# Key and query projections change places between slots, and value evacuations go ahead of a copy, in a decoder layer's cross-attention

## The reference

```
x = layernorm(x + self_attention(x))            # 16 heads of 64, no mask
x = layernorm(x + cross_attention(x, ctx))      # 16 heads of 16, ctx is 8 x 375 x 256, one mask 112 x 375
x = layernorm(x + ffn(x))                       # 8 experts of hidden 512, top-1 by argmax, plus one shared expert

# cross_attention
q = heads(x @ Wq.T + bq); k = heads(ctx @ Wk.T + bk); v = heads(ctx @ Wv.T + bv)
scores = where(mask == 0, -1e10, q k^T / 4); out = softmax(scores) v
return out @ Wo.T + bo
```

## Time and profile before

| | |
|---|---|
| median of 3 runs | 441.21 us (440.41 to 441.44) |
| profiled execution, its own time | 441.44 us |
| span of its trace | 439.7 us |
| TensorE busy (matmuls) | 415.9 us, 95% of the span |
| TensorE busy (weight loads) | 296.5 us, 67% |
| VectorE busy | 245.2 us, 56% |
| ScalarE busy | 194.1 us, 44% |
| GpSimd busy | 50.5 us, 11% |
| TensorE's granted clock, mean | 0.996 |

### The profile page before, as it was taken

How to read it: one execution, slowest core, us unless ns; L and a number is a source line. 1 busy time by engine, 2 the same in 40 slices (tenths; PEclk the granted TensorE clock), 3 DMA queues, 4 the chain that set the end, 5 groups by cost and what they waited for, 6 DMA issues and landing times.

```text
span 439.7 us, 8960 instructions
## 1 busy us (share of the span) xinstructions
PE 415.9 (95%) x3125; PEld 296.5 (67%) x3126; DVE 245.2 (56%) x724; ACT 194.1 (44%) x580; POOL 50.5 (11%) x77
## 2 busy tenths in 40 slices
PE   8999999999999978999999999999989998999992
PEld 7766868788686755777776677667665474666661
DVE  1275756756566565667575666667763452234442
ACT  1163352434426445677567666667673101011110
POOL 3010010101101001000010101010100045212222
PEclk9999999999999999999999999999999999999998
DMA  8998000000000013040404040920000013122210
GB/s 255 363 388 241 1 1 1 0 1 2 1 1 0 1 37 144 1 180 1 180 2 180 12 170 13 364 92 1 1 2 1 1 49 108 46 63 68 58 44 33
DMA packets 15241, 34.22 MB, mean 78 GB/s; under 512 B 2381, under 2 KB 9150, under 8 KB 13920
## 3 DMA queue, kind: packets, MB, share of 16 engines
q1 hardware_dynamic: 13952, 30.70, 20.0%
q0 software_dynamic: 1104, 2.76, 1.8%
q10 hardware_dynamic: 144, 0.23, 0.2%
HBM read 27.24 MB, written 6.70 MB: 77 GB/s over the span
## 4 chain that ended last, share of the span: by engine, by line
PE 66%; issue 23%; DVE 6%; ACT 2%; SPq 1%; DMA 0%; POOLq 0%; POOL 0%; DVEq 0%; ACTq 0%
PE bank L434 9%; PE bank L635 7%; PE bank L504 6%; PE bank L448 6%; PE bank L617 4%; PE bank L880 4%; PE bank L856 4%; PE bank L532 3%; PE bank L491 3%; PE bank L862 3%; PE bank L465 3%; PE bank L526 3%; PE bank L477 3%; PE bank L651 3%; PE bank L518 1%
## 5 line engine op out<-in xcount | busy, mean ns | idle before, releaser
L1232 DVE CUSTOM_DVE_ANT_0 p<-bank,mask 112x375 f32<-112x375 f32 x128 | 62.7, 545 | 38.6 <-PE bank L617 38.6
L996 ACT ACTIVATE p<-p,nm 112x375 f32<-112x375 f32 x128 | 74.8, 609 | 6.0 <-DVE nm L1232 6.0
L635 PEld LDWEIGHTS bank<-ident,p 112*125 112x125 f32 x384 | 48.9, 187 | 22.8 <-issue 13.7
L1003 ACT ACTIVATE pT<-bank 125x336 f32<-125x336 f32 x96 | 42.8, 447 | 46.1 <-PE bank L635 46.1
L635 PE MATMUL bank<-ident,p 112*125 112x112 f32 x384 | 58.8, 286 | 0.9
L434 PE MATMUL bank<-x2T,arena 128*128 128x224 f32 x256 | 53.9, 359 | 0.0
L939 ACT ACTIVATE p<-bank,nm 112x112 f32<-112x112 f32 x128 | 43.6, 366 | 18.6 <-DVE nm L1106 18.6
L434 PEld LDWEIGHTS bank<-x2T,arena 128*128 128x128 f32 x256 | 47.4, 194 | 0.6 <-DMA x2T<-in_xT 0.4
L349 POOL TENSOR_TENSOR rstd<-veps,minus_half 128x1 f32<-128x1 f32 x14 | 7.7, 549 | 297.2 <-DVE veps L1132 297.2
L1099 DVE TENSOR_SCALAR arena<-bank 128x448 f32<-128x448 f32 x32 | 20.0, 624 | 26.5 <-PE bank L434 26.5
L617 PE MATMUL bank<-kT,qz 32*112 32x375 f32 x256 | 28.8, 517 | 3.5 <-ACT x2T L965 2.1
(11 more groups left out here) (140 smaller groups left out, 598.0 us busy)
## 6 DMA issues: line engine op xcount, KB each, us to landing
arena<-in_ug SPq DMA_DIRECT2D x8, 1024.0 KB, 5.8
arena<-in_dn SPq DMA_DIRECT2D x8, 512.0 KB, 7.7
mid<-in_ctxT SPq DMA_DIRECT2D x8, 375.0 KB, 3.1
slots_s<-blank SPq DMA_DIRECT2D x14, 128.5 KB, 3.4
arena<-in_wqk SPq DMA_DIRECT2D x7, 256.0 KB, 4.9
slots_x<-blank SPq DMA_DIRECT2D x14, 128.0 KB, 6.9
p<-slots_s SPq DMA_DIRECT2D x9, 128.5 KB, 2.1
kT<-slots_x SPq DMA_DIRECT2D x9, 128.0 KB
```

The costliest lines, as they stand in the source:

```text
L635: mm = pe.transpose(PE_T2[r][0:SK, t * S:(t + 1) * S], p2[i % RING][:, t * SK:(t + 1) * SK], ident[0:S, 0:S])
L996: act.activation(p2[i % RING], p2[i % RING], ACT.Exp, bias=nm2[:, i % H:i % H + 1], scale=-1.0).then_inc(exp2, 1)
L1003: act.activation(pT2[0:SK, i % RING], PE_T2[r][0:SK, 0:KT * S].rearrange("p (k n) -> p k n", k=KT), ACT.Copy).then_inc(pt2_act, 1)
L1232: v.tensor_tensor_reduce(p2[i % RING], PE_S2[r][0:S, 0:S2], bias[:], 1.0, 3e38, ALU.add, ALU.min, accum_out=nm2[:, i % H:i % H + 1]).then_ ...
```

## The change

Four edits, all in the cross-attention, and all of order. In batches 2 and 4 TensorE's query projection moves from place 2 of (b,1) to place 0, and VectorE's evacuation of it goes ahead of the maximum of strip 3. The second key half moves from place 0 of (b,1) to place 2, in batches 2 and 4 behind a wait for the query's evacuation. On ScalarE the evacuation of the second key half moves from the middle of (b,1) to the front of (b,2). On VectorE what `between(n, 3)` holds, which is the value evacuations (and in slot (0,0) the first part of a layernorm), goes ahead of `evac_pt2`.

```diff
--- before.py
+++ after.py
@@ -713,18 +713,19 @@
                     else:
                         pe.wait_ge(y2, b - 2)
                     project_k(0, b + 1)
-                if (g, place) == (1, 0) and 1 <= b < B - 1:
+                if (g, place) == (1, 0) and b in (2, 4):
                     pe.wait_ge(k_sb, (b + 1) * KC + 1)
-                    project_k(1, b + 1)
+                    project_q(b // 2 + 1)
                 if (g, place) == (1, 1) and b >= 3:
                     turn_x2(b - 3)
-                if (g, place) == (1, 2) and b in (2, 4):
-                    pe.wait_ge(k_sb, (b + 2) * KC)
-                    project_q(b // 2 + 1)
-                if (g, place) == (2, 0) and b >= 1:
+                if (g, place) == (1, 2) and 1 <= b < B - 1:
                     if b in (2, 4):
                         pe.wait_ge(q_sb, b // 2 + 2)
-                    elif b + 1 < B:
+                    else:
+                        pe.wait_ge(k_sb, (b + 1) * KC + 1)
+                    project_k(1, b + 1)
+                if (g, place) == (2, 0) and b >= 1:
+                    if b + 1 < B:
                         pe.wait_ge(k_sb, (b + 2) * KC)
                     else:
                         pe.wait_ge(y2, B - 3)
@@ -1008,8 +1009,8 @@
                 b, g = n // GROUPS, n % GROUPS
                 if b == 0 and g >= 2:
                     evac_x1(g + 2)
-                if g == 1 and 1 <= b < B - 1:
-                    evac_k(0, b + 1)
+                if g in (1, 2) and 1 <= b < B - 1:
+                    evac_k(g - 1, b + 1)
 
             def between(n, place):
 
@@ -1018,8 +1019,6 @@
                     evac_k(1, 1)
                 if (g, place) == (1, 0) and b == 0:
                     evac_x1(3)
-                if (g, place) == (1, 0) and 1 <= b < B - 1:
-                    evac_k(1, b + 1)
                 if (g, place) == (3, 0) and b == 0:
                     evac_x1(6)
                 if (g, place) == (1, 1) and b >= 3:
@@ -1274,7 +1273,7 @@
                     evac_v(2, b, PE_L2)
                 if (g, place) == (1, 0) and b >= 3:
                     ln2_b(b - 3)
-                if (g, place) == (1, 4) and b in (2, 4):
+                if (g, place) == (1, 2) and b in (2, 4):
                     evac_q(b // 2 + 1)
                 if (g, place) == (2, 2) and b == 0:
                     evac_q(1)
@@ -1295,9 +1294,9 @@
                 mask_and_max(n, 2)
                 between(n, 2)
                 mask_and_max(n, 3)
+                between(n, 3)
                 if n >= 1:
                     evac_pt2(n - 1)
-                between(n, 3)
                 between(n, 4)
             ln2_a(NT - 2)
             ln2_b(NT - 2)
```

## The result

The changed kernel takes 445.14 us (median of 6 runs, 444.38 to 445.47), the kernel before 440.68 beside it (6 runs). The ratio is 1.0095 [1.0083, 1.0107]: 0.95% slower. The forecast was 446.6, 1.2% over the 441.21 then known. The sign was right; the size was too large, outside the ratio's interval. The measured median lies 0.2 us above the lower end of the range, and before's 440.68 times 1.0095, 444.87, just under it. Part of the distance is the baseline: the forecast started from 441.21 and expected 5.4 us more; the two medians differ by 4.5 us.

What follows compares the result with a forecast made beforehand. The prediction took TensorE to bound the kernel; 3.7 + 0.5 + 0.1 + 1.1 = 5.4 us on the profiled 441.44 gave 446.8, forecast as 446.6 since that execution lay 0.23 above the median; range 444.9 to 448.2.

Steps and rivals of the forecast that it cites:

- The copy behind the evacuation: VectorE, nine slots: strip 3's copy, now behind the value evacuation, holds up the next scores; 3.7 us slower in all.
- the scores are let go 0.41 us later: End of each of nine slots: copy ends 0.84 us after the evacuation's start, against 0.43, delaying the scores by 0.41.
- (0,2): Slot left out of the copy's cost: evacuation was itself late, so the pair would end at the same time either way.
- The hole in (b,1): TensorE between transposes, batches 1, 3, 5, 6: moving the key projection opens 0.49 us; net plus 0.5 and 0.1 us.
- (1,1): Slot whose key projection moves to place 2: new length 4.78 us against 4.30, plus 0.48.
- The wait for the query evacuation: TensorE in (2,1) and (4,1): key projection waits for VectorE's query evacuation; plus 0.54 us each, 1.1 in all.
- ScalarE's key evacuation at the front of (b,2): ScalarE, second key half ahead of the exponentials: hidden, costs nothing; without cover up to 0.57 us in six slots.
- A: Rival at the slot ends: the copy does not release the scores, so its reordering is free; 442.9 us; 8%.
- C: Rival for TensorE's slots: length is the sum of its work, the hole no wait; 1.4 us less, 439.8; 5%.
- B: Rival in (3,1), (5,1), (6,1): x2's evacuation stays late, 0.5 us waiting kept beside the new hole; 448.1 us; 7%.

Runs made afterwards that it cites:

- waits_before: Kernel before, with TensorE's waits ahead of the scores reordered: value or x2 evacuation first, then the two transpose-copy counts; 439.29 us, ratio 0.9964.
- waits_after: Changed kernel, with TensorE's waits ahead of the scores reordered: value or x2 evacuation first, then the two transpose-copy counts; 446.42 us, ratio 1.0123.
- k0_early: Kernel before, with the next batch's first key half moved from place 2 of (b,0) to place 0, b = 1 to 6; 438.05 us, ratio 0.9946.
- moves: Changed kernel, with VectorE's order of value evacuation and strip 3 copy put back as before; 442.97 us, ratio 1.0041 to the kernel before.
- v_first: Kernel before, with only VectorE's value evacuation put ahead of the copy of strip 3; 442.25 us, ratio 1.0040.
- defer: Kernel before, with only ScalarE's second key evacuation moved to the front of (b,2) for batches 3, 5 and 6; 440.09 us, ratio 0.9992.

## Why the prediction was right in kind, and where it was not

**The copy behind the evacuation: right in place and kind, the size too large.** Nine places were named and nine are there. The copy's end is 0.41 us after the evacuation's, as derived. The failed step is "the scores are let go 0.41 us later". It took the 0.25 us of the earlier trace rows to hold behind any releaser. Behind the copy it is 0.10, as its wait stands one place further in front (`waits_before`, `waits_after`). The scores of (5,3) stood 0.94 us behind the start of the evacuation (287.78-286.84), where 1.1 was forecast and 0.68 would have meant no change. The term of 3.7 us measured 2.41; with the copy's wait third (`waits_after`) it measured 3.72. In (0,3) and (1,3) the scores stood 0.21 behind the evacuation, so the delay is 0.41-0.11 = 0.30. For the same reason (0,2) became 0.16 shorter: the pair ends at the same time, but now the copy ends it. Counted as nothing, that is the second part of the miss.

**The hole in (b,1): right.** `k0_early` and the hardly changed 5.05 of (5,1) show it. The changed kernel's slot (5,1):

```profile
277.92 0.90 PE L617 MATMUL bank<-kT,qz 32*112 32x375 f32 x8
280.63 0.43 PE L676 MATMUL bank<-ident,xres 128*128 128x128 f32 x2
280.90 1.43 PE L526 MATMUL bank<-mid,wx 128*128 128x375 f32 x4
281.87 0.39 ACT L966 ACTIVATE x2T<-bank 128x256 f32<-128x256 f32 x1
282.26 0.78 PE L651 MATMUL bank<-pT,v 125*32 125x112 f32 x24
282.97 0.90 PE L617 MATMUL bank<-kT,qz 32*112 32x375 f32 x8
```

Place 1 comes at 2.71, x2's evacuation is over at 4.34 and the scores don't wait for it. (1,1) cost 0.57, not 0.48: from the key projection to the value products it was 195.53-194.07 = 1.46, while the 1.36 of the earlier trace rows is that of a projection which followed another without a pause.

**The wait for the query evacuation: right, a little too small.** Slot (2,1) of the changed kernel:

```profile
211.57 0.90 PE L617 MATMUL bank<-kT,qz 32*112 32x375 f32 x8
214.87 1.28 DVE L1173 SCALAR_TENSOR_TENSOR qz<-bank,cols,qscale 128x448 f32<-128x448 f32 x2 [0.66 <-PE bank L518]
216.29 1.50 PE L526 MATMUL bank<-mid,wx 128*128 128x375 f32 x4 [0.82 <-DVE qz L1173]
217.73 0.78 PE L651 MATMUL bank<-pT,v 125*32 125x112 f32 x24
```

TensorE goes on at 4.72 where the earlier trace rows gave 4.64, and the projection again takes 1.44 before the next group. Together 1.33 us for a term of 1.1, within its bounds.

**The rest.** ScalarE's key evacuation at the front of (b,2) cost nothing: no slot (b,2) of `moves` changed by more than 0.03. Rivals A and C fall with `v_first` and `k0_early`. B did not come, though `defer` shows its thought was sound: with the transposes later, x2's evacuation is late again. In the changed kernel they are not later.

The slots give 4.09 us, the profiled spans 3.7, since the cross-attention started 0.34 us earlier in that execution; the medians give 4.5.

## What to carry to other kernels

On a saturated in-order engine, moving a piece of work away from between a producer and its consumer's answer uncovers the round trip, even if the total work is the same; look first for slots where nothing stands there, since filling them was worth 2.8 us here. On a helper engine put what is ready ahead of what must wait, when the main engine wants both. And a gap measured behind one releaser is not the latency behind another: where several waits stand before one instruction, try the one that is met last at the front, which was the cheapest place here; at the end it cost 0.14 us in some slots and 0.42 in another.

## What the runs showed that was not expected

With four waits on different semaphores before one TensorE instruction, the time from the end of the last releaser to the instruction was 0.05 us where the unmet wait stood first, 0.10 second, 0.25 third, 0.14 fourth, and 0.20 as third of five. With six waits it was 0.10 as second, 0.21 as third (0.26 in one slot of two of the runs) and 0.36 to 0.42 as fourth. Why is open. Turning the order round was worth 1.54 us of slots in this kernel, 0.36% in the runs. A group of matmuls that starts after a wait took some 0.1 us more until the next group than one that follows another directly (1.44 to 1.46 against 1.36).
